# Splitting the first input block of a one-core test-time-memory and mixture-of-experts kernel into two halves, with the value product ahead of z1's

## The reference, cut to what matters

```python
# x: 2048 tokens x 128; sandwich: x + LN(attn(LN(x))), then x + LN(ffn(LN(x)))
keys    = x @ Wk + bk;  queries = x @ Wq + bq;  values = x @ Wv + bv
alr     = MAX_ALR * sigmoid(x @ Wlr + blr)
# h = h + silu(h @ W + b), for (W1, b1), then (W2, b2); loss against the values, weighted by alr
grads      = jax.grad(loss_fn)(((W1, b1), (W2, b2)))
new_params = tree_map(adamw, params, grads)
retrieved  = _lmm(new_params, queries)
...
# ffn: layernorm, router (top 2 of 8 experts), exact gelu experts, weighted sum
```

## Time and profile before

| | |
|---|---|
| three runs | 186.67, 187.81, 188.04 us; median 187.81 |
| profiled execution | 188.26 us, of which 186.5 us from the first to the last instruction |
| mean granted TensorE clock | 0.986 of full |
| PE / PEld busy | 171.7 / 138.4 us (92% / 74%) |
| DVE / ACT / POOL busy | 136.3 / 96.7 / 25.2 us |

### The profile page before, as it was taken

One profiled execution on the slowest core, in us unless ns is written; L12 is line 12 of the kernel. 1 busy time (PEld: TensorE's weight loads), 2 busy tenths in 40 slices (PEclk: granted clock), 3 DMA queues, 4 the chain that ended last, 5 costly groups with the idle time before them and its releaser, 6 DMA issues.

```text
span 186.5 us, 3118 instructions
## 1 busy us (share of the span) xinstructions
PE 171.7 (92%) x1036; PEld 138.4 (74%) x1036; DVE 136.3 (73%) x541; ACT 96.7 (52%) x169; POOL 25.2 (14%) x36
## 2 busy tenths in 40 slices
PE   6789999998999978996999999999999999999970
PEld 6644456666655347995989999999899999999960
DVE  0987998999584946399346979956979956538693
ACT  3048885957467589322825353826353725535511
POOL 1450000000003530024000024200024200002011
PEclk9969999999999999999999999999999999999998
DMA  4990000000000000000000000010000100000100
GB/s 134 344 307 15 7 4 0 0 0 2 4 0 0 0 0 2 4 0 0 0 4 0 2 0 4 12 44 0 4 2 0 54 7 0 0 4 2 56 28 28
DMA packets 3423, 4.99 MB, mean 27 GB/s; under 512 B 336, under 2 KB 1744, under 8 KB 3408
## 3 DMA queue, kind: packets, MB, share of 16 engines
q1 hardware_dynamic: 3408, 4.81, 8.2%
HBM read 3.76 MB, written 1.05 MB: 26 GB/s over the span
## 4 chain that ended last, share of the span: by engine, by line
PE 72%; DVE 15%; issue 4%; ACT 3%; DMA 2%; POOL 1%; DVEq 0%; ACTq 0%; POOLq 0%
PE bank L375 66%; PE bank L383 4%; DVE stats L852 3%; DMA x_tok<-in_x_dram 2%; DVE mv L855 2%; POOL rstd L328 1%; DVE xn_tok L1009 1%; PE bank L528 1%; DVE xn_tok L865 1%; PE bank L519 1%; DVE h_tok L865 1%; ACT L769 1%; DVE vpe L860 1%; DVE xnT L1087 1%; DVE xnT L1104 1%
## 5 line engine op out<-in xcount | busy, mean ns | idle before, releaser
L1104 DVE SCALAR_TENSOR_TENSOR xnT<-bank,w_tok,xnT 128x128 f32<-128x128 f32 x112 | 31.5, 343 | 21.5 <-PE bank L375 20.8
L328 POOL TENSOR_TENSOR rstd<-vpe,minus_half 128x4 f32<-128x4 f32 (+1 forms) x24 | 21.7, 912 | 116.2 <-DVE vpe L860 105.0
L375 PE MATMUL bank<-z_hi,fW_hi 128*128 128x512 f32 x64 | 27.8, 434 | 0.3 <-ACT alrT L665 0.3
L375 PE MATMUL bank<-z_lo,fW_hi 128*128 128x512 f32 x64 | 25.0, 393 | 0.0
L375 PE MATMUL bank<-z_hi,fW_lo 128*128 128x512 f32 x64 | 25.0, 390 | 0.0
L375 PEld LDWEIGHTS bank<-fW_sb,sig 128*128 128x128 f32 x192 | 23.1, 192 | 0.8
L375 PE MATMUL bank<-fW_sb,sig 128*128 128x128 f32 x192 | 23.4, 275 | 0.0
L788 ACT ACTIVATE sig<-bank,early_sb 128x512 f32<-128x512 f32 x24 | 16.0, 685 | 9.8 <-PE bank L375 9.8
L375 PEld LDWEIGHTS bank<-fW_sb,k_tok 128*128 128x128 f32 x160 | 19.5, 191 | 0.8
L375 PEld LDWEIGHTS bank<-fW_sb,h1T 128*128 128x128 f32 x160 | 19.4, 191 | 0.8
L375 PE MATMUL bank<-fW_sb,k_tok 128*128 128x128 f32 x160 | 19.6, 275 | 0.0
(11 more groups left out here) (131 smaller groups left out, 272.1 us busy)
## 6 DMA issues: line engine op xcount, KB each, us to landing
x_tok<-in_x_dram SPq DMA_DIRECT2D x4, 256.0 KB, 4.5
fW_raw<-in_fW_dram SPq DMA_DIRECT2D x1, 1024.0 KB, 8.5
out_dram<-xn_tok SPq DMA_DIRECT2D x3, 256.0 KB, 2.5
early_sb<-in_early_dram SPq DMA_DIRECT2D x1, 268.0 KB, 4.2
late_sb<-in_late_dram SPq DMA_DIRECT2D x1, 264.0 KB, 4.9
b_raw<-in_late_dram SPq DMA_DIRECT2D x16, 4.0 KB
out_dram<-xn_tok SPq DMA_DIRECT2D x2, 128.0 KB, 1.9
fW_sb<-in_fW_dram SPq DMA_DIRECT2D x1, 0.5 KB, 10.8
```

The lines of the kernel that those rows point to most:

```text
L328: pool.tensor_tensor(rstd[:, ln, where], vpe[:, ln, where], minus_half[:, 0:where.stop - where.start], ALU.pow).then_inc(rstd_ready[ln], 1)
L375: return pe.matmul(out_, lhsT, rhs, start=start, stop=stop)
L1104: last = dve.scalar_tensor_tensor(out=y_tok[:, t, :], in0=bank[Y_BANK[m % len(Y_BANK)]][:, i * P:(i + 1) * P], scalar=w_tok[:, t, e:e + 1] ...
```

## The change

The first block's transfer is cut into two of two tiles each, with a semaphore each (`x_first`). VectorE computes statistics for each half (`first_stats`), GpSimd's power runs for each half, and VectorE normalises them one after the other (`first_norm`); block 1's statistics, which stood between block 0's statistics and its normalising, now follow it. TensorE transposes the halves into two banks (`first_x`, banks 7 and 5), and ScalarE copies each with its own 128x256 activation. These transposes leave the turns of bank 7; the semaphores `first_tr` and `first_out` take their place, and block 1's transposes wait for the first copy. The warm-up is 19 transposes of the identity instead of 28, and two more stand between the halves' transposes and the key product. On TensorE the value product of block 0 is put ahead of z1's, and the transposes of block 1 behind z1's; on ScalarE the copy of block 1's transposes is put behind the first sigmoid.

```diff
-        TURNS = [("x", 0), ("x", 1), ("x", 2)]
+        TURNS = [("x", 1), ("x", 2)]
+        FIRST_BANK = (7, 5)
-        WARM_UP = 28
+        WARM_UP = 19
...
-            load_x(0)
+            for h in range(2):
+                where = slice(h * HALF, h * HALF + HALF)
+                sp.dma_start(x_tok[:, where, :], x_v[:, where, :]).then_inc(x_first[h], 16)
             sp.dma_start(early_sb[:], early).then_inc(early_in, 16)
...
-            rsqrt(LX, 0)
-            rsqrt(LX, 1)
-            rsqrt(LX, 2)
-            rsqrt(LX, 3)
+            rsqrt(LX, 0, slice(0, HALF))
+            rsqrt(LX, 1, slice(HALF, TB))
+            for b in range(1, NB):
+                rsqrt(LX, b + 1, slice(TB * b, TB * b + TB))
...
+            def first_x(h):
+                pe.wait_ge(xn_ready, h + 1)
+                for i in range(HALF):
+                    last = pe.transpose(bank[FIRST_BANK[h]][:, i * P:(i + 1) * P], xn_tok[:, h * HALF + i, :],
+                                        ident[:])
+                last.then_inc(first_tr, 1)
+
             def feature_major_x(b):
-                pe.wait_ge(xn_ready, b + 1)
+                pe.wait_ge(xn_ready, b + 2)
+                if b == 1:
+                    pe.wait_ge(first_out, 1)
...
             def k_product(b):
-                pe.wait_ge(tr_out, turn("x", b) + 1)
                 if b:
+                    pe.wait_ge(tr_out, turn("x", b) + 1)
                     pe.wait_ge(kT_ready, b)
+                else:
+                    pe.wait_ge(first_out, 2)
...
             keep_clock(6, WARM_UP)
-            feature_major_x(0)
+            first_x(0)
+            first_x(1)
+            keep_clock(6, 2)
             pe.wait_ge(early_in, 16)
             k_product(0)
+            v_product(0)
+            z1_product(0)
             feature_major_x(1)
-            z1_product(0)
-            v_product(0)
             k_product(1)
...
-            xnT_out(0)
+            for h in range(2):
+                act.wait_ge(first_tr, h + 1)
+                act.activation(xnT[:, h * HALF * P:(h + 1) * HALF * P], bank[FIRST_BANK[h]][:, 0:HALF * P],
+                               ACT.Identity).then_inc(first_out, 1)
             act.wait_ge(early_in, 16)
             kT_out(0)
+            sig1_out(0)
             xnT_out(1)
-            sig1_out(0)
             nsig1_out(0)
...
+            def first_stats(h):
+                dve.wait_ge(x_first[h], 16)
+                where = slice(h * HALF, h * HALF + HALF)
+                run(statistics(LX, range(where.start, where.stop), lambda i, t: x_tok[:, t, :]))
+                plus_eps(LX, where)
+
+            def first_norm(h):
+                dve.wait_ge(rstd_ready[LX], h + 1)
+                normalise(LX, range(h * HALF, h * HALF + HALF), xn_tok, x_tok, rstd[:, LX, :]).then_inc(xn_ready, 1)
...
-            x_stats(0)
+            first_stats(0)
+            first_stats(1)
+            first_norm(0)
+            first_norm(1)
             x_stats(1)
-            x_norm(0)
             x_stats(2)
             x_norm(1)
```

More of the change, by code:

```diff
@@ L161, in memory_and_experts @@
         x_in = [sem(f"x_in{i}") for i in range(NB)]
+        x_first = [sem(f"x_first{i}") for i in range(2)]
+        first_tr, first_out = sem("first_tr"), sem("first_out")
         early_in, late_in, fw1_in, fw2_in = (sem(n) for n in ("early_in", "late_in", "fw1_in", "fw2_in"))
@@ L874, in x_norm @@
             def x_norm(b):
-                dve.wait_ge(rstd_ready[LX], b + 1)
+                dve.wait_ge(rstd_ready[LX], b + 2)
                 normalise(LX, tiles(b), xn_tok, x_tok, rstd[:, LX, :]).then_inc(xn_ready, 1)
```

## The result

The changed kernel takes 185.63 us (median of 7 runs, 185.49 to 185.72) against 187.81 (7 runs, 186.63 to 188.12): a ratio of 0.991, with a 95% interval of 0.988 to 0.994. The forecast was 186.9, with a range of 186.2 to 188.1. The profiled execution took 185.56 us, its span 183.7, where before had 188.26 and 186.5.

The account below looks back on a forecast made before the run. TensorE was taken to bound the kernel overall, the path to the first sigmoid its start; VectorE's queue would replace that wait, bringing layer1(0) from 15.20 to 13.94, so 188.26 became 187.0, put at 186.9, range 186.2 to 188.1.

Parts of the forecast that it names:

- Part 1: First block's load: split in two transfers, its first half lands at 4.4 us, between 4.0 and 4.70.
- the sum: layer1(0) at 13.94 against 15.20, 1.25 us earlier; from 188.26 profiled this gives 187.0, put at 186.9.
- Parts 2 and 3: VectorE before layer1(0): halves normalised by 6.88 and 7.73; its queue sets layer1(0) at 13.94, replacing the sigmoid wait.
- Part 4: TensorE and ScalarE path to the first sigmoid: key product at 9.05, sigmoid at 12.4 or 15.0 by clock level.
- upper-level case: TensorE at its upper clock level: products of 0.86 us from 9.05, sigmoid done at 12.4.
- Part 5: From layer1(0) to dh1_product(0): TensorE keeps up with 0.6 us of slack, so the shift is kept to the end.
- (d): At dh1_product(0): TensorE's queue, not VectorE, is late at 21.7; up to 0.6 us of gain goes, 187.6; chance 0.08.
- The two groups of before: Three runs of before, 186.67 to 188.04: the spread was read as the clock falling in some runs only.
- (a): Before layer1(0): TensorE's clock comes back between 12.0 and 14.2; gain 0 to 1.25 us, middle 187.6; chance 0.25.
- (b): Low clock lasts beyond z1(0) and delays z2(0): dh1(0) 0.9 us later than before, 189.1; chance 0.10.
- (c): First half lands no sooner, or ScalarE's copies cost more: VectorE's floor 14.25, time 187.3; chance 0.57 together with the forecast.

Follow-up runs that it names:

- the 28-transposes run: Changed kernel with the warm-up at 28 transposes instead of 19: 185.68 us, 185.49 to 186.08, 9 runs.
- the filled kernel before: Kernel before with 32 warm-up transposes instead of 28 and four more ahead of block 0's key product: 186.69 us, 12 runs.
- the halves together: Changed kernel with the second half's transfer issued by ScalarE's queue at the same moment as the first: 187.0 us, 186.61 to 188.25.

## Why the prediction was wrong

**The step that failed is Part 1, the landing of the first half.** "I take 4.4", between 4.0 and 4.70, was worked out from the landing of the whole block less its second half's bytes at the transfer rate. It was 3.10, and that is nearly the whole miss, since `layer1(0)` came 1.26 us before the 13.94 of the sum. The runs show two terms. The second half's bytes were priced near the faster rate (0.37 us); alone in flight, the block lands 0.75 us behind the half, close to what the slower rate gives (0.69). And 0.89 of the 4.70 was not the block's own: with nothing issued behind it the block lands at 3.81. The sum put this wait at nothing. The half does not pay it: it lands as early with the other half and the later loads behind it as alone. Together they are 4.70 - 3.06 = 1.64 us, where the prediction took off 0.3. The lower end of the range, 4.0, left out the second term too, and so was no bound. Why the loads behind it hold back the block and not the half is not shown.

The same part draws on the Trainium skill, "DMA: Bandwidth & Descriptors", section "Anatomy of one DMA". That section is about transfers issued by GpSimd, and these are SyncE's. Its 0.30 us between half and block was 0.75 here.

**Parts 2 and 3 held.** The floor's working with 3.10 in place of 4.4 gives 13.94 - 1.3 = 12.64; measured 12.68. The exposed wait for the second power was 0.33 (0.25 forecast). That the floor of VectorE's queue replaces the wait for the sigmoid is what the timeline and the 28-transposes run show.

**Part 4 held in its upper-level case, but its sum was short.** ScalarE's half copy took 0.38 (0.46 taken). From the key product's start to the sigmoid's end it reckoned 3.35 us (9.05 to 12.4), and it took 3.79 (7.60 to 11.39). The 0.86 us of a product is the spacing of products in a row; one that is waited for takes 1.13 from start to end (z1 at 9.54), and the path waits for two. With the half at 3.10 the sigmoid is out 1.3 us ahead of the floor all the same. The value product ahead of z1's cost nothing, as said; whether it gained anything stays open with the four late runs of the other order (186.68 to 190.98).

**Part 5 held with less slack.** I had 0.6 us of slack on TensorE at `dh1_product(0)`; it was 0.23 (its transposes end at 20.19). The shift of 2.52 passed whole, so (d) fell.

**The sum.** Its form is right: profiled time less the start of `layer1(0)` is 173.06 before, 172.88 after, and 172.8 to 173.1 in every variant but the one that reorders VectorE behind it. The two groups of before were read rightly, as the filled kernel before shows; but the step from 187.0 to 186.9 used the median of a sample of three that fell mostly in the upper group. On the four chips of the experiments the median of before lay anywhere from 186.74 to 187.87, by how many of its runs fell into each of the three groups.

**Rivals.** (a) did not happen in the profiled run of the changed kernel: the transposes came at 5.66 right behind the warm-up (forecast: 6.94, a pause of 1.3 us). Where the half lands late (the halves together) or the warm-up is cut to 8 it does happen, in profiled runs of 187.98 and 186.59. I had tied the clock to the landing without seeing that the same error moved both. (b), at 189.1, is not among the changed kernel's seven runs. (c) was the wrong way round: copies and landing were better, not worse.

## What to carry to other kernels

When a first transfer lands late, part of its time can belong to what is in flight beside it. The landing of the whole less the bytes of a part then says too little about when the part lands: measure the part, or the whole, with nothing behind it. A split pays only together with a consumer that starts on the first part and an order of its queue that lets it. The early half without that order brought 0.15 us or less here (without any consumer the kernel was 0.4% slower), the order without the early half nothing, both together 1.06. And before a change is priced against a median, see whether the runs stand in groups, and whether the mean granted clock goes with them; holding the clock up with fillers in both kernels takes the groups out and leaves the change.

## What the runs showed of the hardware that I had not expected

The page's granted clock reads 1.00 until the trace's first entry for the clock, whatever the level is. In the run with 8 transposes that entry comes at 11.82 us (6.12 in the changed kernel), and the stretch from 7.86 to 11.60 reads 1.00 while its two products take 3.75 us, where the changed kernel's take 1.95. The row of windows (engines' busy us, then clock, DMA share, GB/s):

```profile
7.86:11.60 3.74, 3.74 (x5) 1.63 (x6) 3.04 (x18) 0.69 (x1) 2.04 (x2) 1.00 0.99 327
```

Durations of a known shape tell the level there; the column doesn't. Nor does the mean of a run: the profiled run of the halves together, at 187.98 us, has 0.995. In the profiled run of the kernel before the fall, from 10.58 to 13.99, lies behind the first entry (7.16), so there the mean shows it.

Two transfers of 128 KB issued at the same moment on two queues, with the weights 0.44 us behind, land like one of 256 KB, at 4.35 and 4.53 us. Issued 0.43 us apart on one queue, the first lands at 3.06 to 3.11 in six of seven profiles.
